# Half of a matrix's block sums move to GpSimd, and the first chunk's split, degree rows and seeds of step 0 get places of their own

## Chip, cores, metric

One core of one Trainium2 chip. The time is the device time of one execution in microseconds (us), the median of three runs. The engines are PE (TensorE), DVE (VectorE), ACT (ScalarE), POOL (GpSimd) and SP (SyncE, which here issues DMAs only).

## What is computed

A gated graph network in five steps on 2048 nodes with 256 features, with a random 0/1 adjacency matrix, then a two-layer head, a residual and a layer norm:

```python
Af = A.astype(prop_state.dtype)
AfT = Af.T
state = prop_state
for _ in range(N_STEPS):                       # 5
    s_in = state @ in_W.T + in_b
    s_out = state @ out_W.T + out_b
    a_in = Af @ s_in
    a_out = AfT @ s_out
    a = jnp.concatenate([a_in, a_out, state], axis=-1)
    r = jax.nn.sigmoid(a @ r_W.T + r_b)
    z = jax.nn.sigmoid(a @ z_W.T + z_b)
    joined = jnp.concatenate([a_in, a_out, r * state], axis=-1)
    h_hat = jnp.tanh(joined @ h_W.T + h_b)
    state = (1.0 - z) * state + z * h_hat
out = jnp.tanh(state @ o1_W.T + o1_b) @ o2_W.T + o2_b
...
x = _layernorm(x + out, axis=-1)
```

## The kernel before

The state lives in SBUF transposed (`state_t`, features on partitions, 2048 nodes in four chunks of 512). The adjacency matrix and its transpose are loaded once as int32, in 16 row blocks each (`load_rows(k)`, k from 0 to 31, on SP's queue, 1 MB each, into a ring of three stages in `tmp`), and cast by ACT to fp8 in `areg` (`cast_rows`). A load may start when the cast three rows earlier is done.

**Step 0** multiplies plainly. While the rows arrive, PE multiplies them with the state (first matrix, results "q0"; second, "p0"), with 16 matmuls to a row block, and after the last cast it finishes the p0 banks one after another. Two f16 halves are taken of each result: the upper by ACT, the lower by DVE (`lo_of_psum`). Row and column degrees come from the casts' accumulators: DVE writes them into diagonal matrices (`make_diag(d)`, 16 instructions), PE spreads them over the partitions (`spread_degrees`), and copies of that are `deg`. From `deg` ACT sets a start value in each gate bank (`seed`), and DVE adds the second matrix's part (`degree_part`). `split_hi` on ACT and `split_lo` on DVE give the halves of the state. Then `gates(0, c)` computes r, z and h for each chunk, in six tiles of 18 matmuls.

**Later steps** use Strassen's scheme on 2 x 2 blocks, which needs sums of the matrix's blocks. These don't change from step to step. They are formed once, by `matrix_sums(i)`: a job i is one pair of row blocks of one of the two matrices (0 to 7 the first, 8 to 15 the second) and takes four fp8 TENSOR_TENSORs of 128 x 1024. Its result goes to DRAM (`kept`), from where `load_group` brings each group's operands back on SP's queue. In the kernel before, DVE forms all sixteen jobs: 0 to 3 while the first matrix is loaded, 4 to 7 behind the q0 splits, 8 to 10 before `make_diag(1)`, 11 to 14 one in each chunk of `gates(0, c)`, and 15 behind them. POOL issues all the stores. Jobs 0 to 10 use three slots in `xop_words` (`ring_a`), the others two in `tmp` (`ring_b`).

Each engine runs its program in the order in which it is written, and semaphores (`wait_ge`, `then_inc`) tie them together. `s_cast` counts the casts, `s_t` the jobs.

## Time and profile before

| | |
|---|---|
| median of three runs | 1091.42 us (1090.13 to 1094.82) |
| profiled execution | 1092.24 us, its span 1090.2 us |
| PE busy | 1034.3 us of the span |
| DVE, ACT, POOL busy | 599.2, 412.0 and 37.7 us |
| granted TensorE clock, mean | 0.976 of full speed |

The span goes from the first to the last instruction. A busy share is an average over stages with different limits. The first 144 us are the loading stage, from there to about 252 us the gates of step 0 run, and the rest is four later steps and the head.

### The profile page before, as it was taken

Reading aid. Unit: us, or ns where it says so; the run is one execution under the profiler, and the core shown is the slowest. Engines: PE = TensorE matmul, PEld = TensorE weight load, DVE = VectorE, ACT = ScalarE, POOL = GpSimd, SP = SyncE. Lnnn points to the kernel's source line nnn. Section 1 sums busy time; section 2 is a strip of 40 time slices with the busy share of each in tenths; the row PEclk is TensorE's granted clock in tenths of the full one; section 3 lists DMA queues with packets and bytes.
Section 4 is the critical chain, followed back from the end, with each engine's and each line's share of the span. In section 5 each row is a group of like instructions: output and inputs, shape, how many; then the busy total and the mean of one; then the engine's idle time right before and its main releaser. Section 6 shows DMA issues by size and latency. Waiting matters only on the chain.

```text
span 1090.2 us, 11726 instructions
## 1 busy us (share of the span) xinstructions
PE 1034.3 (95%) x4776; PEld 476.2 (44%) x4776; DVE 599.2 (55%) x938; ACT 412.0 (38%) x546; POOL 37.7 (3%) x44
## 2 busy tenths in 40 slices
PE   7999979998799999999999999999999999998983
PEld 3444434443344444444444444444444444444441
DVE  5999847777244337543533664353356435355546
ACT  4655545452134116522421552242155214212431
POOL 0311000000000000000000000000000002001100
PEclk8999989999899999999999999999999999999997
DMA  9999960000630032033003301400330043000101
GB/s 344 396 368 377 385 221 20 20 20 26 283 135 1 1 145 127 1 118 152 1 1 135 136 1 69 183 20 0 135 136 1 18 184 113 1 24 15 39 1 39
DMA packets 28869, 119.63 MB, mean 110 GB/s; under 512 B 2064, under 2 KB 17040, under 8 KB 20624
## 3 DMA queue, kind: packets, MB, share of 16 engines
q1 hardware_dynamic: 26512, 110.51, 26.3%
q0 software_dynamic: 2304, 8.39, 1.9%
q8 instruction: 37, 0.61, 0.2%
q14 instruction: 16, 0.13, 0.0%
HBM read 102.11 MB, written 16.78 MB: 109 GB/s over the span
## 4 chain that ended last, share of the span: by engine, by line
PE 87%; DVE 6%; ACT 2%; DMA 2%; issue 2%; SPq 1%; DVEq 0%; ACTq 0%
PE bank L1118 41%; PE bank L1030 32%; PE bank L973 10%; PE bank L1140 1%; PE bank L1131 1%; DMA areg<-kept_operands 1%; DMA tmp<-in_adj 1%; PE bank L1159 1%; DVE areg L845 1%; DVE split L710 1%; ACT xop_words L427 0%; DVE ln_st L837 0%; DVE deg_words L699 0%; DVE tmp L634 0%; DVE tmp L631 0%
## 5 line engine op out<-in xcount | busy, mean ns | idle before, releaser
L1030 PE MATMUL bank<-areg,xop_words 128*128 128x512 fp8e4 x1792 | 393.6, 382 | 6.9 <-DMA areg<-kept_operands 5.5
L1118 PE MATMUL bank<-pq_words,w 128*128 128x512 f16 x1440 | 330.2, 382 | 0.0
L1030 PEld LDWEIGHTS bank<-areg,xop_words 128*128 128x128 f16 x1792 | 175.2, 98 | 220.5 <-DMA areg<-kept_operands 6.0
L1118 PEld LDWEIGHTS bank<-pq_words,w 128*128 128x128 f16 x1440 | 141.6, 98 | 171.2 <-issue 5.0
L435 ACT ACTIVATE tmp<-bank,bias_sb,scal 128x512 f32<-128x512 f32 x120 | 93.3, 778 | 236.6 <-PE bank L1118 228.2
L1118 PE MATMUL bank<-split,w 128*128 128x512 f16 x480 | 120.3, 388 | 15.1 <-DVE bank L735 8.2
L735 DVE SCALAR_TENSOR_TENSOR bank<-deg_words,vdeg,bank 128x512 f32<-128x512 f16 x120 | 90.0, 753 | 64.1 <-ACT bank L449 62.9
L506 ACT ACTIVATE pq_words<-pq_words 128x512 f16<-128x512 f32 x48 | 30.2, 630 | 238.3 <-DVE pq_words L886 142.0
L973 PE MATMUL bank<-areg,xop_words 128*128 128x512 fp8e4 x512 | 113.8, 386 | 3.1 <-ACT areg L375 3.1
L449 ACT ACTIVATE bank<-deg_words,vdeg 128x512 f32<-128x512 f16 x120 | 82.6, 691 | 5.4 <-DVE deg_words L699 1.7
L973 PEld LDWEIGHTS bank<-areg,xop_words 128*128 128x128 f16 x512 | 50.7, 99 | 65.6 <-issue 7.4
L1118 PEld LDWEIGHTS bank<-split,w 128*128 128x128 f16 x480 | 47.2, 99 | 70.3 <-issue 10.3
L375 ACT ACTIVATE areg<-tmp 128x2048 fp8e4<-128x2048 int32 x32 | 61.1, 1911 | 36.9 <-DMA tmp<-in_adj_t 21.5
L741 DVE TENSOR_TENSOR tmp<-tmp,state_t 128x512 f32<-128x512 f32 x40 | 27.7, 692 | 67.2 <-ACT tmp L435 67.2
L1118 PE MATMUL bank<-tmp,w 128*128 128x512 f16 x240 | 58.4, 380 | 0.0
L900 DVE SCALAR_TENSOR_TENSOR pq_words<-pq_words 128x512 f16<-128x512 f32 x48 | 33.2, 693 | 33.4 <-ACT pq_words L506 33.4
L717 DVE SCALAR_TENSOR_TENSOR xop_words<-pq_words,scal,xop_words 128x512 f16<-128x512 f32 (+1 forms) x32 | 36.8, 1151 | 25.4 <-ACT xop_words L427 25.4
L758 DVE TENSOR_TENSOR tmp<-tmp 128x512 f32<-128x512 f32 x40 | 27.6, 691 | 41.5 <-ACT tmp L435 41.5
L358 POOL TENSOR_TENSOR areg<-areg,diag_words 128x256 f32<-128x256 f32 x16 | 14.6, 942 | 735.4 <-DMA areg<-in_x 735.4
L710 DVE SCALAR_TENSOR_TENSOR split<-state_t,scal,split 128x1024 f16<-128x1024 f32 x24 | 30.7, 1283 | 12.3 <-ACT split L406 12.2
L874 DVE TENSOR_TENSOR pq_words<-bank,pq_words 128x512 f32<-128x512 f32 x16 | 11.0, 688 | 45.5 <-PE bank L1030 45.5
L1118 PEld LDWEIGHTS bank<-tmp,w 128*128 128x128 f16 x240 | 23.5, 98 | 28.3
(114 smaller groups left out, 646.6 us busy)
## 6 DMA issues: line engine op xcount, KB each, us to landing
areg<-kept_operands SPq DMA_DIRECT2D x32, 1792.0 KB, 10.7
tmp<-in_adj SPq DMA_DIRECT2D x16, 1024.0 KB, 7.3
tmp<-in_adj_t SPq DMA_DIRECT2D x16, 1024.0 KB, 8.7
kept_operands<-xop_words POOLq DMA_DIRECT2D x11, 512.0 KB, 7.9
areg<-in_x SPq DMA_DIRECT2D x8, 512.0 KB, 8.1
kept_operands<-areg SPq DMA_DIRECT2D x4, 1024.0 KB, 9.6
kept_operands<-tmp POOLq DMA_DIRECT2D x5, 512.0 KB, 3.1
pq_words<-in_gate_w SPq DMA_DIRECT2D x6, 384.0 KB, 5.8
```

What stands on the lines that cost most here:

```text
L375: nc.scalar.activation(raw8[k // JT][:, k % JT, :], stage[:, k % STG, :], ACT.Copy, accum_out=degc[:, k // JT, k % JT:k % JT + 1], saturat ...
L435: nc.scalar.activation(dst[:, gi % FT, :], gate_bank[gi % 3][:, :], ACT.Tanh if gi >= 2 * FT else ACT.Sigmoid, bias=bias_sb[:, 4 + gi:5 + ...
L449: nc.scalar.activation(gate_bank[gi % 3][:, :], deg[:, 0, cols(c)], ACT.Identity, scale=vdeg[:, 0, gi:gi + 1]).then_inc(s_c0, 1)
L506: nc.scalar.activation(dst, src, ACT.Copy, scale=PSC / XDOWN).then_inc(s_yh, 1)
L710: nc.vector.scalar_tensor_tensor(split[:, c % 2, 1, :, :], state_t[:, :, cols(c)], SIG, split[:, c % 2, 0, :, :], ALU.mult, ALU.subtract). ...
L717: nc.vector.scalar_tensor_tensor(xop[:, xs, 1, 2 * c:2 * c + 2, :], stg[:, bs, :], SIGX, xop[:, xs, 0, 2 * c:2 * c + 2, :], ALU.mult, ALU. ...
L735: nc.vector.scalar_tensor_tensor(slot, deg[:, 1, cols(c)], vdeg[:, 1, gi:gi + 1], slot, ALU.mult, ALU.add).then_inc(s_c1, 1)
L741: nc.vector.tensor_tensor(r_buf[:, f, :], r_buf[:, f, :], state_t[:, f, cols(c)], ALU.mult) \
L900: nc.vector.scalar_tensor_tensor(rows[:, 1, :], src, PSC / XDOWN, rows[:, 0, :], ALU.mult, ALU.subtract).then_inc(s_yl, 1)
L973: return nc.tensor.matmul(dst[:, :], state_n[:, j, part, feat(f)], adj8[:, j, cols(c)], start=j == 0 and part == 0, stop=j == JT - 1 and p ...
L1030: last = nc.tensor.matmul(dst[:, :], xop[:, xo, part, m, :], slot8[g % 2][:, m, mo, :], start=first and m == pairs[0] and part == 0, stop= ...
L1118: last = nc.tensor.matmul(dst[:, :], w16[:, k, wp, feat(gi)], rhs, start=False, stop=i == KT - 1 and (wp, xp) == PASSES[-1], skip_group_ch ...
```

## The change

Jobs 8 to 15 are formed by POOL (four `nc.gpsimd.tensor_tensor` each, then the store on its own queue). Jobs 8 to 12 use the second half of `state_t` as two slots (`ring_s`), so the second halves of `x_t` are loaded behind their stores, on SP's queue. Jobs 13 to 15 use `ring_b` and wait for the last cast. DVE keeps jobs 0 to 7; the stores of 4 to 7 are issued by SP, between the loads of rows 24 to 29, each behind a wait for its job. The reduction of `ow` moves ahead of the q0 splits. The split of chunk 0 moves up: on ACT behind the cast of row 26, on DVE ahead of `make_diag(1)`. ACT copies the degree rows of the first matrix and DVE those of the second; seeds wait for one bank each; and the splits of p0 for chunks 2 and 3 come behind them.

```diff
-RING_A = 11
-GATE_JOBS = len(TJOBS) - RING_A
+EARLY_JOBS = 4
+RING_S = 13
...
+        ring_s = state_t[:, :, N // 2:]
...
+        def sums_slot(i):
+            if i < PAIRS:
+                return ring_a[:, i % 3, :], s_kept_a[i], 0
+            if i < RING_S:
+                return ring_s[:, (i - PAIRS) % 2, :], s_kept_s[(i - PAIRS) % 2], (i - PAIRS) // 2
+            return ring_b[:, (i - RING_S) % 2, :], s_kept_b[(i - RING_S) % 2], (i - RING_S) // 2
+
+        def sums_parts(i):
+            d, m = TJOBS[i]
+            t = [sums_slot(i)[0].bitcast(F8).rearrange("p (h s n) -> p h s n", h=2, s=4)[:, :, s, :]
+                 for s in range(4)]
+            even, odd = [raw8[d][:, 2 * m + e, :].rearrange("p (h q n) -> p h q n", h=2, q=2) for e in range(2)]
+            return t, even, odd
+
+        def sums_home(i):
+            d, m = TJOBS[i]
+            return kept.rearrange("(h d) p m w -> d p h m w", d=2)[d][:, :, m, MT1 * CW // 4:]
...
-                if k == JT + 1:
+                if k == JT - 4:
                     sp.dma_start(ow, o_w.rearrange("(k p) m -> p k m", p=P)).then_inc(s_ow, 16)
-                if k in (11, 15, 19, 23):
-                    f, part = (k - 11) // 8, (k - 11) // 4 % 2
-                    ns = slice(part * N // 2, (part + 1) * N // 2)
-                    sp.dma_start(state_t[:, f, ns], x_t[f * P:(f + 1) * P, ns]).then_inc(s_xt[f], 16)
+                if k in (13, 15):
+                    f = (k - 13) // 2
+                    sp.dma_start(state_t[:, f, 0:N // 2], x_t[f * P:(f + 1) * P, 0:N // 2]).then_inc(s_xt[f], 16)
+                if k in (JT + 8, JT + 9, JT + 10, JT + 12):
+                    i = EARLY_JOBS + (JT + 8, JT + 9, JT + 10, JT + 12).index(k)
+                    sp.wait_ge(s_t, i + 1)
+                    sp.dma_start(sums_home(i), sums_words(i)).then_inc(sums_slot(i)[1], 16)
...
             store_raw(0)
             store_raw(1)
+            for f in range(FT):
+                for i in range(2):
+                    sp.wait_ge(s_kept_s[i], 16 * len(range(PAIRS + i, RING_S, 2)))
+                sp.dma_start(state_t[:, f, N // 2:], x_t[f * P:(f + 1) * P, N // 2:]).then_inc(s_xt[f], 16)
             sp.wait_ge(s_q0, 2 * CH)
             sp.wait_ge(s_t, PAIRS)
             sp.wait_ge(s_raw[0], 64)
+            for i in range(PAIRS):
+                sp.wait_ge(s_kept_a[i], 16)
             load_group(1, 0)
-            sp.wait_ge(s_t, 2 * PAIRS)
+            sp.wait_ge(s_tp, PAIRS)
             sp.wait_ge(s_raw[1], 64)
+                sp.wait_ge(s_kept_b[i], 16 * len(range(RING_S + i, len(TJOBS), 2)))
             load_group(1, 1)
...
-            def store_sums(i):
-                d, m = TJOBS[i]
-                to = kept.rearrange("(h d) p m w -> d p h m w", d=2)[d][:, :, m, MT1 * CW // 4:]
+            for i in range(EARLY_JOBS):
                 pool.wait_ge(s_t, i + 1)
-                if i < RING_A:
-                    nc.gpsimd.dma_start(to, ring_a[:, i % 3, :].rearrange("p (h w) -> p h w", h=2)) \
-            for i in range(PAIRS):
-                store_sums(i)
+                nc.gpsimd.dma_start(sums_home(i), sums_words(i)).then_inc(sums_slot(i)[1], 16)
             pool.wait_ge(s_mx, 3)
             nc.gpsimd.partition_all_reduce(mall[:, 3:5], mx[:, 3:5], P, RMAX).then_inc(s_mall, 1)
+
+
             for i in range(PAIRS, len(TJOBS)):
-                store_sums(i)
+                (t1, t2, t3, t4), even, odd = sums_parts(i)
+                slot, kept_sem, uses = sums_slot(i)
+                n = i - PAIRS
+                pool.wait_ge(s_cast, JT + 2 * n + 2)
+                if i == RING_S:
+                    pool.wait_ge(s_cast, 2 * JT)
+                if uses > 0:
+                    pool.wait_ge(kept_sem, 16 * uses)
+                nc.gpsimd.tensor_tensor(t1, even[:, :, 1, :], even[:, :, 0, :], ALU.subtract, saturate=False) \
+                    .then_inc(s_tcp, 1)
+                nc.gpsimd.tensor_tensor(t3, odd[:, :, 1, :], even[:, :, 1, :], ALU.subtract, saturate=False)
+                pool.wait_ge(s_tcp, 2 * n + 1)
+                nc.gpsimd.tensor_tensor(t2, odd[:, :, 1, :], t1, ALU.subtract, saturate=False).then_inc(s_tcp, 1)
+                pool.wait_ge(s_tcp, 2 * n + 2)
+                nc.gpsimd.tensor_tensor(t4, odd[:, :, 0, :], t2, ALU.subtract, saturate=False).then_inc(s_tp, 1)
+                pool.wait_ge(s_tp, n + 1)
+                nc.gpsimd.dma_start(sums_home(i), sums_words(i)).then_inc(kept_sem, 16)
...
-            for k in range(JT + 1, 2 * JT):
-                cast_rows(k)
-            for c in range(CH):
-                for f in range(FT):
-                    act.wait_ge(s_p0, 2 * c + f + 1)
-                    nc.scalar.activation(pq[:, c, f, 0, :], bank[p0_bank(c, f)][:, :], ACT.Copy, scale=PSC) \
-                        .then_inc(s_p0h, 1)
-
 
             def split_hi(c, at, new):
+                if at == 0:
+                    for f in range(FT):
+                        act.wait_ge(s_xt[f], 16)
+                if at == 2:
+                    for f in range(FT):
+                        act.wait_ge(s_xt[f], 32)
...
+            for k in range(JT + 1, 2 * JT):
+                cast_rows(k)
+                if k == JT + 10:
+                    split_hi(0, 0, 0)
             act.wait_ge(s_bias, 16)
-            act.wait_ge(s_deg, 2 * CH)
+            for c in range(CH // 2):
+                for f in range(FT):
+                    p0_hi(c, f)
+            for c in range(CH):
+                act.wait_ge(s_dg, c + 1)
+                nc.scalar.copy(deg[:, 0, cols(c)], bank[4 + c][:, :]).then_inc(s_deg_in, 1)
+            act.wait_ge(s_deg_in, CH)
             for gi in range(3):
+                act.wait_ge(s_deg_out, gi + 1)
                 seed(0, 0, gi)
-            for f in range(FT):
-                act.wait_ge(s_xt[f], 32)
-            split_hi(0, 0, 0)
+            for c in range(CH // 2, CH):
+                for f in range(FT):
+                    p0_hi(c, f)
...
             def matrix_sums(i):
-                d, m = TJOBS[i]
-                words = ring_a[:, i % 3, :] if i < RING_A else ring_b[:, (i - RING_A) % 2, :]
-                dve.wait_ge(s_cast, JT * d + 2 * m + 2)
-                if 3 <= i < RING_A:
-                    dve.wait_ge(s_kept_a[i % 3], 16 * (i // 3))
-                if i >= RING_A + 2:
-                    dve.wait_ge(s_kept_b[(i - RING_A) % 2], 16 * ((i - RING_A) // 2))
-                nc.vector.tensor_tensor(t1, even[:, :, 1, :], even[:, :, 0, :], ALU.subtract, saturate=False).then_inc(s_tc, 1)
+                (t1, t2, t3, t4), even, odd = sums_parts(i)
+                dve.wait_ge(s_cast, 2 * i + 2)
+                if i >= 3:
+                    dve.wait_ge(s_kept_a[i - 3], 16)
+                nc.vector.tensor_tensor(t1, even[:, :, 1, :], even[:, :, 0, :], ALU.subtract, saturate=False) \
+                    .then_inc(s_tc, 1)
...
-            for c in range(CH):
-                for f in range(FT):
-                    dve.wait_ge(s_q0h, 2 * c + f + 1)
-                    lo_of_psum(c, FT + f, bank[2 * c + f], s_q0l)
-            for i in range(4, PAIRS):
-                matrix_sums(i)
-            make_diag(0)
-
             dve.wait_ge(s_ow, 16)
             nc.vector.tensor_reduce(mx[:, 3:4], ow[:, :, 0:D], mybir.AxisListType.XY, ALU.max,
                                     apply_absolute_value=True)
             nc.vector.tensor_reduce(mx[:, 4:5], ow[:, :, D:2 * D], mybir.AxisListType.XY, ALU.max,
                                     apply_absolute_value=True).then_inc(s_mx, 1)
+
+            for c in range(CH):
+                for f in range(FT):
+                    dve.wait_ge(s_q0h, 2 * c + f + 1)
+                    lo_of_psum(c, FT + f, bank[2 * c + f], s_q0l)
+            for i in range(EARLY_JOBS, PAIRS):
+                matrix_sums(i)
+            make_diag(0)
+
...
-            for i in range(PAIRS, RING_A):
-                matrix_sums(i)
-            make_diag(1)
-
-            def p0_lo(c, f):
-                dve.wait_ge(s_p0h, 2 * c + f + 1)
-                lo_of_psum(c, f, bank[p0_bank(c, f)], s_p0l)
-
-            def deg_out(d):
-                for c in range(CH):
-                    dve.wait_ge(s_dg, CH * d + c + 1)
-                    nc.vector.tensor_copy(deg[:, d, cols(c)], bank[4 + c][:, :]).then_inc(s_deg, 1)
-
-            for c in range(CH):
-                p0_lo(c, 0)
-                if c >= CH - 2:
-                    deg_out(c - (CH - 2))
-                p0_lo(c, 1)
-            dve.wait_ge(s_deg, 2 * CH)
-
             def split_lo(c, at):
                 dve.wait_ge(s_sph, at + 1)
                 nc.vector.scalar_tensor_tensor(split[:, c % 2, 1, :, :], state_t[:, :, cols(c)], SIG,
                                                split[:, c % 2, 0, :, :], ALU.mult, ALU.subtract).then_inc(s_spl, 1)
+
+            split_lo(0, 0)
+            make_diag(1)
+
+            def p0_lo(c, f):
+                dve.wait_ge(s_p0h, 2 * c + f + 1)
+                lo_of_psum(c, f, bank[p0_bank(c, f)], s_p0l)
+
+            for c in range(CH // 2):
+                for f in range(FT):
+                    p0_lo(c, f)
+            for c in range(CH):
+                dve.wait_ge(s_dg, CH + c + 1)
+                nc.vector.tensor_copy(deg[:, 1, cols(c)], bank[4 + c][:, :]).then_inc(s_deg_out, 1)
+            dve.wait_ge(s_deg_out, CH)
...
                 keep_part(n, c, 1)
-                if t == 0:
-                    for i in range(RING_A + c, RING_A + c + 1):
-                        matrix_sums(i)
...
-            split_lo(0, 0)
+            for c in range(CH // 2, CH):
+                for f in range(FT):
+                    p0_lo(c, f)
             for c in range(CH):
                 gates(0, c)
-                if c == CH - 1:
-                    for i in range(RING_A + CH, len(TJOBS)):
-                        matrix_sums(i)
...
                     else:
-                        pe.wait_ge(s_deg, c + 1)
+                        pe.wait_ge(s_deg_in, c + 1)
                     nc.tensor.matmul(bank[4 + c][:, :], ones[:, :], diag[d][:, c * JC:(c + 1) * JC, :],
                                      start=True, stop=True).then_inc(s_dg, 1)
```

On SP, between the loads of the second matrix, before (the rows of `in_adj_t` are rows 16 to 31; `x_t` goes to `state_t`):

```order
L250 DMA tmp<-in_adj_t 128x2048 [waits s_cast] x2
L264 DMA state_t<-in_x_t 128x1024
L250 DMA tmp<-in_adj_t 128x2048 [waits s_cast] x4
L264 DMA state_t<-in_x_t 128x1024
L250 DMA tmp<-in_adj_t 128x2048 [waits s_cast] x8
L274 DMA kept_operands<-areg 1024x1x128 [waits s_cast]
```

and after, with the four stores of DVE's jobs (`kept_operands<-xop_words`) among the loads:

```order
L274 DMA tmp<-in_adj_t 128x2048 [waits s_cast] x9
L291 DMA kept_operands<-xop_words 128x2x512 [waits s_t]
L274 DMA tmp<-in_adj_t 128x2048 [waits s_cast]
L291 DMA kept_operands<-xop_words 128x2x512 [waits s_t]
L274 DMA tmp<-in_adj_t 128x2048 [waits s_cast]
L291 DMA kept_operands<-xop_words 128x2x512 [waits s_t]
L274 DMA tmp<-in_adj_t 128x2048 [waits s_cast] x2
L291 DMA kept_operands<-xop_words 128x2x512 [waits s_t]
L274 DMA tmp<-in_adj_t 128x2048 [waits s_cast] x3
L301 DMA kept_operands<-areg 1024x1x128 [waits s_cast]
```

The two late loads of `state_t` are gone from here. Four waits for `s_t` stand ahead of the last seven loads.

On DVE, from the last sums or the splits of the output weights (`o`) to the first gate seeds, before:

```order
L634 TENSOR_TENSOR xop_words<-areg,xop_words 128x2x512 [waits s_tc]
L636 TENSOR_TENSOR xop_words<-areg,xop_words 128x2x512 [waits s_tc]
L645 TENSOR_SCALAR tmp<-ident,degc 128x128 [waits s_cast]
L645 TENSOR_SCALAR tmp<-ident,degc 128x128 x15
L639 SCALAR_TENSOR_TENSOR pq_words<-bank,pq_words 128x512 [waits s_p0h] x5
L699 CAST deg_words<-bank 128x512 [waits s_dg] x4
L639 SCALAR_TENSOR_TENSOR pq_words<-bank,pq_words 128x512 [waits s_p0h] x2
L699 CAST deg_words<-bank 128x512 [waits s_dg] x4
L639 SCALAR_TENSOR_TENSOR pq_words<-bank,pq_words 128x512 [waits s_p0h]
L735 SCALAR_TENSOR_TENSOR bank<-deg_words,vdeg,bank 128x512 [waits s_c0,s_deg]
L735 SCALAR_TENSOR_TENSOR bank<-deg_words,vdeg,bank 128x512 [waits s_c0] x2
L710 SCALAR_TENSOR_TENSOR split<-state_t,scal,split 128x1024 [waits s_sph]
```

and after:

```order
L664 SCALAR_TENSOR_TENSOR o<-deg_words,scal,o 128x2x256 [waits s_wh]
L736 SCALAR_TENSOR_TENSOR split<-state_t,scal,split 128x1024 [waits s_sph]
L690 TENSOR_SCALAR tmp<-ident,degc 128x128 [waits s_cast]
L690 TENSOR_SCALAR tmp<-ident,degc 128x128 x15
L684 SCALAR_TENSOR_TENSOR pq_words<-bank,pq_words 128x512 [waits s_p0h] x4
L751 CAST deg_words<-bank 128x512 [waits s_dg] x4
L776 SCALAR_TENSOR_TENSOR bank<-deg_words,vdeg,bank 128x512 [waits s_c0,s_deg_out]
L776 SCALAR_TENSOR_TENSOR bank<-deg_words,vdeg,bank 128x512 [waits s_c0] x2
L684 SCALAR_TENSOR_TENSOR pq_words<-bank,pq_words 128x512 [waits s_p0h] x4
```

The split of chunk 0 (`split<-state_t`) went from behind the seeds to ahead of the diagonal matrix (`tmp<-ident,degc`). One of two sets of degree copies (CAST) stays, the sums (`xop_words<-areg,xop_words`) are gone, and half of the p0 splits follow the seeds.

On POOL, behind the first four stores, before (the all-reduce is the ISA row):

```order
L335 ISA areg<-areg 128x1536 [waits s_vpart]
L342 DMA kept_operands<-xop_words 128x2x512 [waits s_t] x8
L351 ISA mall<-mx 128x2 [waits s_mx]
L342 DMA kept_operands<-xop_words 128x2x512 [waits s_t] x3
L345 DMA kept_operands<-tmp 128x2x512 [waits s_t] x5
```

and after, the first of eight jobs:

```order
L367 DMA kept_operands<-xop_words 128x2x512 [waits s_t] x4
L369 ISA mall<-mx 128x2 [waits s_mx]
L381 ISA
L381 TENSOR_TENSOR state_t<-areg 128x2x512 [waits s_cast]
L383 TENSOR_TENSOR state_t<-areg 128x2x512
L385 TENSOR_TENSOR state_t<-areg,state_t 128x2x512 [waits s_tcp]
L387 TENSOR_TENSOR state_t<-areg,state_t 128x2x512 [waits s_tcp]
L389 DMA kept_operands<-state_t 128x2x512 [waits s_tp]
```

Stores that only waited for DVE have become POOL's own sums, each with its store behind it.

## Rows read from the trace of the kernel before

**Rows 1.** The page: each engine's busy time and share of the span.

```profile
PE 1034.3 (95%) x4776; PEld 476.2 (44%) x4776; DVE 599.2 (55%) x938; ACT 412.0 (38%) x546; POOL 37.7 (3%) x44
```

**Rows 2.** Stretch: us, busy PE, PEld, DVE, ACT, POOL; clock, DMA share, GB/s.

```profile
100.00:110.00 10.00, 10.00 (x48) 4.50 (x47) 9.01 (x35) 4.56 (x5) 1.09 (x2) 1.00 1.02 427
```

**Rows 3.** Timeline of ACT (start, us, what): two casts.

```profile
79.59 1.90 ACT L375 ACTIVATE areg<-tmp 128x2048 fp8e4<-128x2048 int32 x1
...
125.03 1.91 ACT L375 ACTIVATE areg<-tmp 128x2048 fp8e4<-128x2048 int32 x1 [2.65 <-DMA tmp<-in_adj_t]
```

**Rows 4.** The chain of waits, 120 to 150 us (start, us, what).

```profile
131.76 0.60 ACT pq_words L397
...
142.18 1.29 DVE split L710
```

**Rows 5.** Timeline of PE, with idle time before and what ended it.

```profile
143.60 2.72 PE L1118 MATMUL bank<-split,w 128*128 128x512 f16 x6 [6.82 <-DVE split L710]
...
150.37 1.46 PE L1118 MATMUL bank<-split,w 128*128 128x512 f16 x6
...
200.33 2.45 PE L1118 MATMUL bank<-split,w 128*128 128x512 f16 x6 [2.31 <-DVE bank L735]
...
252.44 1.12 PE L1131 MATMUL bank<-ident,state_t 128*128 128x128 f32 x4 [3.29 <-DVE state_t L761]
...
285.37 14.89 PE L1030 MATMUL bank<-areg,xop_words 128*128 128x512 fp8e4 x59 [5.47 <-DMA areg<-kept_operands]
```

**Rows 6.** Timelines of SP's queue and of POOL: issues of DMAs.

```profile
116.44 0.33 SPq L250 DMA_DIRECT2D tmp<-in_adj_t  x1
...
274.19 6.54 SPq L283 DMA_DIRECT2D areg<-kept_operands  x4
...
270.91 0.72 POOL L345 DMA_DIRECT2D kept_operands<-tmp  x1 [18.82 <-DVE tmp L636]
```

**Rows 7.** Timeline of DVE in the loading stage.

```profile
76.76 4.88 DVE L639 SCALAR_TENSOR_TENSOR pq_words<-bank,pq_words 128x512 f16<-128x512 f32 x8
81.55 1.22 DVE L631 TENSOR_TENSOR xop_words<-areg 128x1024 fp8e4<-128x1024 fp8e4 x1
82.68 1.23 DVE L632 TENSOR_TENSOR xop_words<-areg 128x1024 fp8e4<-128x1024 fp8e4 x1
...
101.02 2.69 DVE L645 TENSOR_SCALAR diag_words<-ident,degc 128x128 f16<-128x128 f16 x16
...
110.11 1.22 DVE L631 TENSOR_TENSOR xop_words<-areg 128x1024 fp8e4<-128x1024 fp8e4 x1
```

**Rows 8.** Timelines of POOL and of DVE around 914 us.

```profile
0.24 0.10 POOL L1217 MEMSET const-float32-0.0<- 128x1 f32 x1 [0.24 <-issue]
...
913.41 0.72 POOL L358 TENSOR_TENSOR areg<-areg,diag_words 128x256 f32<-128x256 f32 x1
914.09 1.18 POOL L358 TENSOR_TENSOR areg<-areg,diag_words 128x256 f32<-128x256 f32 x1
915.23 1.17 POOL L358 TENSOR_TENSOR areg<-areg,diag_words 128x256 f32<-128x256 f32 x1
...
914.71 1.10 DVE L761 TENSOR_TENSOR state_t<-tmp 128x512 f32<-128x512 f32 x1
...
918.53 0.69 DVE L761 TENSOR_TENSOR state_t<-tmp 128x512 f32<-128x512 f32 x1
```

**Rows 9.** DVE beside POOL, by timeline, and the page's line of L735.

```profile
910.76 0.76 DVE L735 SCALAR_TENSOR_TENSOR bank<-deg_words,vdeg,bank 128x512 f32<-128x512 f16 x1 [0.40 <-ACT bank L449]
...
983.62 0.43 DVE L823 TENSOR_SCALAR pq_words<-pq_words 128x512 f16<-128x512 f32 x1 [4.00 <-ACT pq_words L482]
...
984.70 0.95 DVE L823 TENSOR_SCALAR pq_words<-pq_words 128x512 f16<-128x512 f32 x1
...
37.46 6.59 DVE L604 TENSOR_TENSOR scal<-scal,mall 128x1 f32<-128x1 f32 x1
...
L735 DVE SCALAR_TENSOR_TENSOR bank<-deg_words,vdeg,bank 128x512 f32<-128x512 f16 x120 | 90.0, 753 | 64.1 <-ACT bank L449 62.9
```

More of the change, by code:

```diff
@@ L160, in gnn_program @@
         s_p0, s_p0h, s_p0l = sem("s_p0"), sem("s_p0h"), sem("s_p0l")
-        s_diag, s_dg, s_deg = sem("s_diag"), sem("s_dg"), sem("s_deg")
-        s_tc, s_t = sem("s_tc"), sem("s_t")
-        s_kept_a = [sem(f"s_kept_a{i}") for i in range(3)]
+        s_diag, s_dg, s_deg_in, s_deg_out = sem("s_diag"), sem("s_dg"), sem("s_deg_in"), sem("s_deg_out")
+        s_tc, s_t, s_tcp, s_tp = sem("s_tc"), sem("s_t"), sem("s_tcp"), sem("s_tp")
+        s_kept_a = [sem(f"s_kept_a{i}") for i in range(PAIRS)]
         s_kept_b = [sem(f"s_kept_b{i}") for i in range(2)]
+        s_kept_s = [sem(f"s_kept_s{i}") for i in range(2)]
         s_raw = [sem("s_raw0"), sem("s_raw1")]
@@ L421, in rows_hi @@
                     if n == 0:
-                        for i in range(3):
-                            act.wait_ge(s_kept_a[i], 16 * len(range(i, RING_A, 3)))
+                        for i in range(PAIRS):
+                            act.wait_ge(s_kept_a[i], 16)
                 else:
@@ L646, in make_diag @@
                 last.then_inc(s_diag, 1)
-            for i in range(4):
+            for i in range(EARLY_JOBS):
                 matrix_sums(i)
@@ L686, in _, with split_lo @@
                 split_raw(3 + i, [o16[:, :, h, ms] for h in range(2)], ow[:, :, ms], om)
-            for i in range(PAIRS, RING_A):
-                matrix_sums(i)
+            def split_lo(c, at):
+                dve.wait_ge(s_sph, at + 1)
+                nc.vector.scalar_tensor_tensor(split[:, c % 2, 1, :, :], state_t[:, :, cols(c)], SIG,
+                                               split[:, c % 2, 0, :, :], ALU.mult, ALU.subtract).then_inc(s_spl, 1)
+            split_lo(0, 0)
             make_diag(1)
@@ L1126, in transposes @@
                 if n == 0 and f == 0:
-                    pe.wait_ge(s_deg, 2 * CH)
+                    pe.wait_ge(s_deg_out, CH)
                     pe.wait_ge(s_id32, 1)
```

23 lines of the change are left out of this document (6 added, 17 removed).

## The prediction

> **What bounds the kernel now.** I read the engines' busy time first. TensorE (PE) is busy 95% of the span [rows 1], so only what makes PE wait, or a gap that closes, can move the time. The change touches the first 300 us, so I read that part by stretches. From 100 to 110 us, as in the stretches around it, PE is busy throughout, DVE nine tenths, and the DMA engines are saturated (share 1.02 at 427 GB/s) [rows 2]: adjacency rows arrive, ACT casts them, PE multiplies them. The three run neck and neck. The last cast starts at 125.03 and ends at 126.9 [rows 3], and PE's last block of the stage can only start then.
>
> Then I read the chain of waits from 130 to 144 us and PE's idle time. Behind the last block stand degree copies, seeds and the split of chunk 0, one after another on DVE and ACT [rows 4], and PE idles 6.8 us before its first gate matmul at 143.60 [rows 5]. It then runs at its lower clock: six matmuls take 2.72 us where six take 1.46 later [rows 5], which is about 3 us over the first tile. Inside step 0 PE waits 2.3 us (once more like it, at 228.68) and 3.3 us for what DVE does behind `matrix_sums` [rows 5]. At 285.37 it waits 5.5 us for the load of group 1 [rows 5], which SP issued at 274.19, after the last job had been stored at 270.91 [rows 6]. So about 17 us of idle time plus some 5 us of slow clock lie open: 22 us at most.
>
> **What the change moves, without any interference.** The eight jobs of the second matrix leave DVE. A job there is four TENSOR_TENSORs at 1.13 us from start to start [rows 7], 4.6 us. Three of them stood before the end of the stage, where DVE had slack anyhow, and four stood in step 0. The split of chunk 0, the seeds and half of the degree copies leave the gap: the chain after the last block shrinks from 11.9 us to about 7, of which PE's last block covers most. I put the gates at 139.8 instead of 143.6 (the moved reduction of `ow`, 1.3 us for two of them, sits before the eight q0 splits, which hold PE's next pass, and costs 0.9 us). Step 0 loses another 6 us of waits, and the wait at 285 goes with its slow clock after it (59 matmuls in 14.89 us, where 48 took 10.00 [rows 2] and 59 would take 12.5): 7.5 us. The sum is -3.8 - 6 - 7.5, about -17 us.
>
> **What POOL costs.** No row shows POOL on fp8. The nearest are its 256-element additions: 0.72 us alone at 913.41, the next starting 0.68 us later [rows 8]. Four times that gives 2.7 us for a 1024-element instruction. Less if a part is fixed: a one-element MEMSET takes 0.10 [rows 8], so (0.68 - 0.1) x 4 + 0.1 = 2.4. A job on POOL is then 4 x 2.3 plus 0.72 for its DMA issue, 10 us, against 4.6 on DVE. From the cast that job 8 needs (the one from 79.59 to 81.5 [rows 3]) five jobs end near 131, three more near 161. `load_group(1, 1)` and the second halves of `state_t` (needed some 40 us into the gates) are in time. By itself the slower engine is hidden.
>
> **What is not hidden: the two engines block each other.** The same POOL additions took 1.18 and 1.17 us when DVE worked on SBUF beside them, and the DVE instruction between them 1.10 instead of 0.69 [rows 8]. They follow one another strictly: POOL's starts are 914.09 and 915.23, 1.14 apart instead of 0.68. The DVE instruction holds about half of the 1.13 that one of twice the elements takes [rows 7], which leaves 0.57 to POOL. Instructions with one operand in PSUM are free of it (L735 took 0.76 while POOL worked, its mean over all 120 is 753 ns) [rows 9]. A TENSOR_SCALAR from SBUF to SBUF is not: 0.95 against 0.43 [rows 9]. Even a one-element TENSOR_TENSOR waited 6.59 us beside the all-reduce [rows 9]. And `make_diag`'s sixteen, 2.69 us together [rows 7], are of the TENSOR_SCALAR kind.
>
> The Trainium skill ("SBUF — State Buffer", section "Who interferes with whom") has this as a rule: a DVE instruction with two SBUF inputs, or one in a two-port mode, excludes a GpSimd instruction that reads SBUF, and whichever comes second is blocked until the first ends. By this rule, the trace agrees, the change's two streams of block sums run in turn and not side by side; without the blocking the sum would be the -17 us above, with it the +17 below. The skill's "GPSIMD Engine Reference" (section 3) gives 4497 ns for a 2048-element addition there; an estimate from it is 2.3 us for 1024, which would leave the sum as it is.
>
> For 1024 elements POOL's hold is 0.57 x 4 = 2.3 us, or 0.1 + 0.47 x 4 = 2.0 with a fixed part; I take 2.1. DVE holds 1.1. One turn of both is 3.2 us.
>
> Now the chain. (1) DVE comes to job 4 at 82.9 (81.6 and the 1.3 of the moved reduction), POOL to job 8 at 81.5. Each of DVE's sixteen instructions of jobs 4 to 7 waits for one of POOL's: the jobs end at 94.5, 107, 120 and 133. Before, the last of the four ended where `make_diag(0)` starts, at 101.0 [rows 7]. (2) SP now waits for just these jobs between adjacency loads. Load 26 now stands behind job 5 (107), 27 and 28 behind job 6 (120), 29 to 31 behind job 7 (133). Before, the last was issued at 116.44 and had 8.6 us to its cast [rows 3, 6]; three loads and two stores, 4 MB, take 10 us at 427 GB/s and 2 to land: the last cast ends at 147, 20 us late. (3) DVE goes on from 133 with the sixteen of `make_diag(0)`, and POOL's job 12 puts four turns between them: 133 + 2.6 + 8.4 = 144 less what has run already, 143. Scales and `o16` splits (what lies between the end of `make_diag(0)` and 110.11 [rows 7], less the moved reduction: 5.1 us) bring it to 148, the split of chunk 0 to 151. (4) At the last cast, 147, POOL starts jobs 13 to 15, just as DVE comes to `make_diag(1)`. Of POOL's twelve instructions about seven fall between DVE's twenty-one short ones: 148 + 1.2 + 2.6 + 7 x 2.1 = 166. (5) PE waits there for the second degree rows. Behind it on DVE come four splits (2.4), four degree copies (2.4), a seed on ACT (0.7) and its other half (0.8), with 1.5 for semaphores and matmuls: the gates start at 174, 30 us later than at 143.6. (6) Then -6 us in step 0 and -7.5 at the wait for group 1: 30 - 13.5 = 16.5 us.
>
> PE loses its clock in the long waits, but what it then does slowly lies under DVE's chain, and the first gate tile was slow before as well, so I add nothing. The profiled execution has a span of 1090.2 and a time of 1092.24, 0.8 over the median of 1091.42. **1092.2 + 16.5 is 1109 us.** The sum is steep: 16 + 4 + 7 = 27 POOL instructions lie on the path, so a hold of 2.0 gives 1105, of 2.3 gives 1121, and at 1.5 the change breaks even.
>
> **Rivals.** *No blocking* (fp8 work or its modes don't meet): all is hidden and the sum is -17, 1075 us. For it: what met in the trace was f32 and f16, not fp8. Against it: [rows 8, 9]. Chance 0.20. *POOL's fp8 instructions are short*, 1.0 to 1.4 us, since four elements share a word: same turns, jobs 4 to 7 end by 116 to 121, last cast 131 to 137, and the sum is -10 to -3: 1082 to 1089. No row speaks for it. 0.08. *Only long instructions block*, and the short ones of `make_diag` slip through between POOL's: steps 1 and 2 stand, 3 and 4 shrink to 151 for the second diagonal, the gates start at 159: +15 - 13.5, 1088 to 1099. For it: instructions of 0.16 us beside POOL's pause between two. 0.14. *POOL needs 3 us or more* for fp8 conversions: over 1126, with state halves that then arrive late too. 0.04. My forecast, 1100 to 1126, has 0.54.
>
> The bound for a real difference is 0.5% (1086 and 1097). Faster: the first rival and some of the second, 0.25. Same: the rest of it and half of the third, 0.12. Slower: 0.63. With cases of both signs the range reaches from 1077 to 1125, which leaves out half of the first rival, the last one, and the edge of my own.
>
> **What would show it.** In the changed profile: POOL's TENSOR_TENSORs, alone 2.2 to 2.7 us, beside DVE 3.2 apart; DVE's sums 3.2 us from start to start at 84 to 133 (step 1); SP's loads of `in_adj_t` with idle time behind DVE's sums, last cast near 147 (2); `make_diag` stretched from 2.7 to 10 us or more (3, 4); the first gate matmul near 174 (5); no wait for `kept_operands` in group 1, and step 0 without the 2 us waits (6). If DVE's sums stay 1.13 apart I am wrong from step 1 on; if SP's loads are on time, in step 2.

## Result and the profile after

The changed kernel takes 1111.74 us (median of four runs, 1111.67 to 1112.68) against 1093.05 for the kernel before on the same chip (1090.13 to 1094.82). The ratio is 1.0176 with a 95% interval of [1.0148, 1.0203]: slower by 1.8%, 18.7 us. The profiled execution took 1111.69 us with a span of 1109.9.

The page answers to [rows 1]: TensorE's share of the span falls from 95% to 93%, since its own work is the same and the span longer; POOL's busy time grows by 66.5 us.

```profile
PE 1030.0 (93%) x4776; PEld 474.2 (43%) x4776; DVE 618.0 (56%) x902; ACT 413.5 (37%) x550; POOL 104.2 (9%) x72
```

The next table is that of the stretches (us, busy time of PE, PEld, DVE, ACT and POOL; PE clock, DMA share, GB/s) of the changed kernel, cut at the end of the q0 splits, the last casts, the first gate matmul and the end of step 0.

```profile
78.00:127.00 49.00, 38.93 (x176) 16.56 (x174) 48.90 (x21) 19.61 (x21) 40.85 (x21) 0.95 0.61 219
127.00:153.00 26.00, 14.77 (x49) 5.72 (x50) 19.60 (x38) 10.01 (x10) 9.80 (x6) 0.71 0.87 309
153.00:187.00 34.00, 12.14 (x42) 4.31 (x41) 29.53 (x25) 7.50 (x13) 25.48 (x15) 0.70 0.96 337
187.00:283.00 96.00, 96.00 (x460) 45.34 (x458) 60.56 (x88) 54.20 (x74) 0.00 (x0) 1.00 0.09 37
283.00:316.00 33.00, 32.71 (x155) 14.87 (x154) 14.22 (x21) 9.11 (x13) 0.00 (x0) 1.00 0.20 78
```

Of the 109 us from 78 to 187 PE works 66, and DVE is recorded as busy for 98, in the first stretch with 21 instructions in 49 us; time in which an instruction stands and waits for the other engine counts as busy here. The DMA share, 1.02 from 100 to 110 us before [rows 2], is 0.61 over the first stretch: it is no longer the loads that are short of bandwidth. From 187 on PE has no gap at all. The same view of the kernel before, for step 0 and what follows:

```profile
144.00:252.00 108.00, 100.54 (x456) 45.79 (x454) 73.92 (x97) 53.14 (x71) 2.82 (x4) 0.96 0.12 48
252.00:286.00 34.00, 27.54 (x122) 12.55 (x123) 19.20 (x26) 7.25 (x10) 0.81 (x2) 0.90 0.41 160
```

DVE's timeline in the changed kernel (start, us, what; in brackets idle time before and what ended it) shows the sums that [rows 7] has at 1.22 us each:

```profile
83.88 1.21 DVE L679 TENSOR_TENSOR xop_words<-areg,xop_words 128x1024 fp8e4<-128x1024 fp8e4 x1
85.13 2.91 DVE L681 TENSOR_TENSOR xop_words<-areg,xop_words 128x1024 fp8e4<-128x1024 fp8e4 x1
87.97 3.02 DVE L675 TENSOR_TENSOR xop_words<-areg 128x1024 fp8e4<-128x1024 fp8e4 x1
...
96.91 7.14 DVE L681 TENSOR_TENSOR xop_words<-areg,xop_words 128x1024 fp8e4<-128x1024 fp8e4 x1
103.98 3.02 DVE L675 TENSOR_TENSOR xop_words<-areg 128x1024 fp8e4<-128x1024 fp8e4 x1
106.93 7.06 DVE L677 TENSOR_TENSOR xop_words<-areg 128x1024 fp8e4<-128x1024 fp8e4 x1
...
137.95 2.68 DVE L690 TENSOR_SCALAR diag_words<-ident,degc 128x128 f16<-128x128 f16 x16
```

POOL's timeline in the same kernel:

```profile
84.55 2.41 POOL L381 TENSOR_TENSOR state_t<-areg 128x1024 fp8e4<-128x1024 fp8e4 x1 [7.17 <-issue]
...
97.03 2.02 POOL L381 TENSOR_TENSOR state_t<-areg 128x1024 fp8e4<-128x1024 fp8e4 x1
99.00 2.01 POOL L383 TENSOR_TENSOR state_t<-areg 128x1024 fp8e4<-128x1024 fp8e4 x1
100.96 2.00 POOL L385 TENSOR_TENSOR state_t<-areg,state_t 128x1024 fp8e4<-128x1024 fp8e4 x1
103.04 2.88 POOL L387 TENSOR_TENSOR state_t<-areg,state_t 128x1024 fp8e4<-128x1024 fp8e4 x1
106.22 0.73 POOL L389 DMA_DIRECT2D kept_operands<-state_t  x1 [0.30 <-POOL state_t L387]
```

Read the two side by side. DVE's instruction of 96.91 "takes" 7.14 us: it stands there while POOL's of 97.03, 99.00 and 100.96 run, and gets its 1.13 us in ahead of the one of 103.04, which stands itself for that time (2.88 us instead of 2.01). The next one comes in behind that one, at POOL's store. So DVE gets two instructions into each of POOL's jobs of 9.93 us, at the two places where POOL itself waits for something (ahead of its fourth instruction, and for its store), and none between POOL's first three. Between 85 and 96 us it was different: there POOL's instructions took 2.9 to 3.0 us as well and the two engines alternated. The traces of this kernel and of the experiments below that leave POOL's order as it is (x1, x2, y2, y3, z2) sort the two patterns, with one exception: in a job that POOL begins straight behind its store, 0.02 or 0.03 us later, DVE's waiting instruction is passed over, and in a job that POOL begins after a pause of 1 us or more (job 8, later job 13, in x1 job 15) it is let in after one. The exception is y3's job at 171.95. Why it is so, the traces don't show.

The chain of waits, up to the first gate matmul (start, us, what; "issue" is time in which the trace shows no reason to wait):

```profile
136.81 1.24 DVE xop_words L681
...
138.06 0.38 SPq L291
...
139.85 10.51 DMA tmp<-in_adj_t
...
150.38 2.01 ACT areg L411 x2
...
152.41 24.20 DVE tmp L690 x16
...
184.91 1.90 issue
186.81 31.24 PE bank L1155 x144
```

These seven lines hold the delay of the first gate matmul: the last job of DVE ends at 138, SP stores it and issues the last three loads, which before had gone out by 116.44 [rows 6]; they come in, the last cast ends at 152.3 (126.9 before), and `make_diag(1)` takes 24.20 us where sixteen such instructions took 2.69 [rows 7]. The view of its line gives the shortest, median and longest of the sixteen in ns:

```profile
L690 DVE TENSOR_SCALAR tmp<-ident,degc x16: 241/248/6569, 152.4 to 170.0; 128x128 f16<-128x128 f16 x16
```

So most of them pay nothing. One by one, nine took 0.24 or 0.25 us, five 1.99 to 2.04 (one POOL instruction) and two 6.57 (three POOL instructions in a row). PE's timeline, which answers to [rows 5]:

```profile
132.40 8.50 PE L1010 MATMUL bank<-areg,xop_words 128*128 128x512 fp8e4 x32 [15.44 <-ACT areg L411]
...
177.36 2.38 PE L1050 MATMUL bank<-diag_words,ones 128*128 128x512 f16 x4 [19.91 <-DVE pq_words L684]
179.53 3.62 PE L1010 MATMUL bank<-areg,xop_words 128*128 128x512 fp8e4 x8
...
186.81 1.46 PE L1155 MATMUL bank<-split,w 128*128 128x512 f16 x6 [1.90 <-issue]
...
282.67 0.60 PE L1168 MATMUL bank<-ident,state_t 128*128 128x128 f32 x4
```

The gates start 43.2 us late (186.81 against 143.60). Step 0, up to the first transpose behind its gates, takes 95.9 us against 108.8: 13.0 back. The rest of the span takes 827.2 against 837.8: 10.6 back. 43.2 - 13.0 - 10.6 is 19.6 us; the spans differ by 19.7.

### The profile page after: what moved, and what is told of

Same layout as the page of the kernel before. It is cut to its first block, busy times and chain, and to the rows that moved or that the text cites. A ratio compares the mean times of both kernels' runs of the same rounds, so it can differ in the third digit from the quotient of the medians.

```text
span 1109.9 us, 11731 instructions
## 1 busy us (share of the span) xinstructions
PE 1030.0 (93%) x4776; PEld 474.2 (43%) x4776; DVE 618.0 (56%) x902; ACT 413.5 (37%) x550; POOL 104.2 (9%) x72
## 4 chain that ended last, share of the span: by engine, by line
PE 79%; DVE 14%; issue 3%; DMA 2%; ACT 1%; SPq 1%; POOL 0%; DVEq 0%
PE bank L1155 42%; PE bank L1067 33%; DVE tmp L690 2%; DVE xop_words L677 2%; DVE xop_words L675 1%; DVE xop_words L679 1%; PE bank L1168 1%; PE bank L1177 1%; DMA tmp<-in_adj_t 1%; PE bank L1196 1%; DMA areg<-in_x 1%; DVE scal L654 1%; DVE areg L883 1%; DVE xop_words L631 1%; DVE w L664 0%
## 5 line engine op out<-in xcount | busy, mean ns | idle before, releaser
L1155 PE MATMUL bank<-split,w 128*128 128x512 f16 x480 | 118.0, 382 | 5.5 <-DVE bank L776 3.6
L799 DVE TENSOR_TENSOR tmp<-tmp 128x512 f32<-128x512 f32 x40 | 27.8, 695 | 43.2 <-ACT tmp L469 43.2
L461 ACT ACTIVATE xop_words<-pq_words,scal 128x512 f16<-128x512 f32 (+1 forms) x32 | 33.1, 1036 | 7.0 <-DVE pq_words L771 6.5
## 6 DMA issues: line engine op xcount, KB each, us to landing
areg<-kept_operands SPq DMA_DIRECT2D x32, 1792.0 KB, 10.6
```

Of the source, the lines that this page charges most:

```text
L461: nc.scalar.activation(xop[:, xs, 0, 2 * c:2 * c + 2, :], stg[:, bs, :], ACT.Identity, scale=SIGX) \
L1155: last = nc.tensor.matmul(dst[:, :], w16[:, k, wp, feat(gi)], rhs, start=False, stop=i == KT - 1 and (wp, xp) == PASSES[-1], skip_group_ch ...
```

## Experiments

| kernel | us | ratio to before, same chip | gates start |
|---|---|---|---|
| after | 1111.74 | 1.0176 [1.0148, 1.0203] | 186.8 |
| x1_late13 | 1090.25 | 0.9974 [0.9959, 0.9989] | 163.8 |
| x2_stores_behind | 1108.81 | one run | 184.3 |
| x3_pool_writes | 1076.32 | one run | 151.8 |
| x4_pool_chained | 1103.03 | one run | 178.5 |
| y1_chain_only | 1084.50 | 0.9932 [0.9909, 0.9955] | 138.2 |
| y2_pool_five_late | 1075.20 | 0.9848 [0.9822, 0.9874] | 140.1 |
| y3_pool_after_dve | 1088.77 | 0.9970 [0.9953, 0.9987] | 162.4 |
| z1_five_late_chained | 1074.42 | 0.9833 [0.9808, 0.9858] | 138.1 |
| z2_five_late_again | 1077.21 | 0.9866 [0.9842, 0.9890] | 138.0 |

x2, x3 and x4 have one run each, so what is read from them rests on their traces and not on a few us of their times.

My theory, A: DVE's and POOL's instructions exclude each other on SBUF, and both the late loads and the 24 us of `make_diag(1)` come from it. Rivals: the loss is SP's new waits by themselves; or POOL's traffic slows DVE whatever POOL does; or POOL passes DVE over only because its instructions stand back to back (C).

**x1: jobs 13 to 15 wait for `make_diag(1)`.**

```diff
                 if i == RING_S:
                     pool.wait_ge(s_cast, 2 * JT)
+                    pool.wait_ge(s_diag, 2)
```

> One wait added to the changed kernel: POOL starts job 13 only when the second diagonal matrix is done. Theory A (POOL's instructions on SBUF shut out DVE's two-input and two-port ones): the sixteen diagonal writes take 2.7 us again instead of 24.2, the first gate matmul comes at 165 to 169 instead of 186.8, and jobs 13 to 15 then stretch DVE's work in step 0 by 2 to 6 us: 1093 to 1099 us. Theory B (POOL is merely slow, and DVE's instructions are long for another reason, such as the DMA traffic of that stretch, which stays): the diagonal writes stay near 24 us and the time near 1111.

DVE's timeline:

```profile
152.15 2.69 DVE L691 TENSOR_SCALAR tmp<-ident,degc 128x128 f16<-128x128 f16 x16 [5.26 <-ACT areg L412]
```

One wait, on an engine whose results nobody needs yet, gives back 21.5 us: `make_diag(1)` is at its old 2.69, the gates start at 163.8, and the kernel is 0.3% faster than the one before, some 3 us better than I had expected. The last cast ends at 152.0, as late as in the changed kernel. The three jobs now run beside the first chunk of step 0, where the longest DVE instruction they stretched took 2.36 us. So the cost of `make_diag(1)` is that of POOL's jobs beside it.

**x2: SP stores jobs 4 to 7 behind the last load**, so no load waits for a job.

```diff
-                if k in (JT + 8, JT + 9, JT + 10, JT + 12):
-                    i = EARLY_JOBS + (JT + 8, JT + 9, JT + 10, JT + 12).index(k)
+                if k == 2 * JT - 1:
+                  for i in range(EARLY_JOBS, PAIRS):
```

> The changed kernel with the four stores of jobs 4 to 7 issued by SP behind the last load, so that no load waits for a job. Theory A: the last cast ends at 127 to 130 instead of 152, but DVE's jobs still end near 138 and POOL's jobs 13 to 15 now fall on both diagonal matrices and the splits, so the first gate matmul stays within 180 to 192 and the time within 1104 to 1118. Theory B2 (SP's waits are the whole loss): gates from 160 on, 1085 to 1092.

```profile
139.05 26.36 DVE L690 TENSOR_SCALAR diag_words<-ident,degc 128x128 f16<-128x128 f16 x16
...
171.23 2.68 DVE L690 TENSOR_SCALAR tmp<-ident,degc 128x128 f16<-128x128 f16 x16
```

The last cast ends at 122.9, 29 us earlier, and the gates start only 2.5 us earlier. POOL's jobs 13 to 15 now begin as soon as job 12 is stored, at 139, and meet the first `make_diag` instead of the second. Without SP's waits the loads are in time, but this takes away one of two delays of the same origin, and the other one stands. The rival "SP's waits by themselves" falls. The edit has a price of its own: job 7 waits 5.96 us, at 122.29, for the late store of the slot that it writes to, and the 2.5 us hold this too.

**x3: POOL only writes.** Its four subtractions become four MEMSETs into the same places (the sums of the second matrix are left out and zeros stored; the rest is as in the changed kernel).

```diff
-                nc.gpsimd.tensor_tensor(t1, even[:, :, 1, :], even[:, :, 0, :], ALU.subtract, saturate=False) \
-                    .then_inc(s_tcp, 1)
+                nc.gpsimd.memset(first, 0.0).then_inc(s_tcp, 1)
...
```

> POOL's 32 subtractions are replaced by 32 MEMSETs of 2048 fp8 elements each (the sums of the second matrix are left out, zeros are stored). Theory A with the rule that only reads of POOL meet DVE's second input: DVE's sums of jobs 4 to 7 take 1.14 us each again and end near 101 to 105, the loads are in time, while the second diagonal (a two-port kind) is still stretched if POOL's MEMSETs are about 2 us long: 1075 to 1095. Theory A2 (any POOL instruction on SBUF shuts out any of these on DVE): sums of 3 to 7 us as in the changed kernel and 1105 to 1112. Theory B (traffic, not the engines): no change in DVE's durations, 1105 to 1112.

DVE's timeline, then POOL's:

```profile
90.24 1.22 DVE L683 TENSOR_TENSOR xop_words<-areg,xop_words 128x1024 fp8e4<-128x1024 fp8e4 x1
91.38 1.22 DVE L677 TENSOR_TENSOR xop_words<-areg 128x1024 fp8e4<-128x1024 fp8e4 x1
...
105.17 17.18 DVE L692 TENSOR_SCALAR diag_words<-ident,degc 128x128 f16<-128x128 f16 x16
...
128.17 15.08 DVE L692 TENSOR_SCALAR tmp<-ident,degc 128x128 f16<-128x128 f16 x16
```

```profile
90.91 1.82 POOL L384 MEMSET state_t<- 128x2048 fp8e4 x1
92.65 1.82 POOL L386 MEMSET state_t<- 128x2048 fp8e4 x1
```

POOL's four instructions of a job stand back to back, and DVE's subtractions keep their 1.22 us and 1.14 from start to start. The TENSOR_SCALARs do not: 17 and 15 us. So it is not the DMA traffic, which is heavier here (a share of 0.99 from 78 to 127 us) than in the changed kernel (0.61). Two kinds of DVE instruction meet POOL: one with two SBUF inputs meets POOL's subtractions but not its MEMSETs, which read nothing, and the TENSOR_SCALAR meets both. The time of 1076 is no forecast, since the kernel leaves out the sums, but the gates still start 8 us later than in the kernel before, with the last cast on time (127.3) and only `make_diag` stretched.

The Trainium skill ("SBUF — State Buffer", section "Who interferes with whom") states both halves: two SBUF inputs contend with a GpSimd instruction that reads, "not with one that only writes it", and TENSOR_SCALAR can enter the two-port modes, which contend with either. By this rule, the trace agrees: 1.22 us against 3.02, and 17 us against 2.69.

**x4: each POOL subtraction waits for the one before**, so that none stands back to back.

```diff
+                pool.wait_ge(s_tcp, 3 * n + 1)
                 nc.gpsimd.tensor_tensor(t3, odd[:, :, 1, :], even[:, :, 1, :], ALU.subtract, saturate=False)
...
```

> The changed kernel, but each of POOL's four subtractions waits for the one before it. In the changed kernel DVE gets in only where POOL has a wait of its own (before the fourth instruction and at the store), three POOL instructions late otherwise. Theory C (POOL holds on from one instruction to the next when nothing holds it back): DVE gets in behind every instruction, turns of 3.1 us, jobs 4 to 7 end near 134 instead of 138 with no instruction of 7 us, the second diagonal takes 15 to 26 us, 1104 to 1112. Theory D (who comes next has nothing to do with POOL's waits): instructions of 7 us stay.

```profile
109.18 3.04 DVE L683 TENSOR_TENSOR xop_words<-areg,xop_words 128x1024 fp8e4<-128x1024 fp8e4 x1
112.15 3.02 DVE L677 TENSOR_TENSOR xop_words<-areg 128x1024 fp8e4<-128x1024 fp8e4 x1
115.09 3.02 DVE L679 TENSOR_TENSOR xop_words<-areg 128x1024 fp8e4<-128x1024 fp8e4 x1
...
153.31 15.62 DVE L692 TENSOR_SCALAR tmp<-ident,degc 128x128 f16<-128x128 f16 x16
```

The 7 us instructions are gone. DVE and POOL take strict turns of 2.95 us, and the four jobs end at 124 instead of 138, ten us before my forecast for this run. This is the turn-taking that the prediction assumed, and waits between POOL's instructions make it last. C holds so far: with the waits DVE is never passed over. Without them it isn't always, so standing back to back is not the whole condition. `make_diag(1)` shrinks to 15.6 (again seven of the sixteen wait, but each for one POOL instruction), but `make_diag(0)` now meets POOL as well (15.6 us), and so do the splits between the two. In all 8.7 us come back, a little more than I had expected.

**y1: the chain part of the change alone**, put into the kernel before: split, degree rows, seeds and p0 splits in their new places, all jobs on DVE, loads and stores as they were.

```diff
+                if k == JT + 10:
+                    for f in range(FT):
+                        act.wait_ge(s_xt[f], 32)
+                    split_hi(0, 0, 0)
...
+            split_lo(0, 0)
             make_diag(1)
```

> The kernel before with the chain part of the change alone: the split of chunk 0, the degree rows (one matrix on ACT, one on DVE), the seeds' waits and the late half of the p0 splits have their new places; all sixteen jobs stay on DVE where they were, POOL computes nothing, loads and stores are as before. Theory A (all the loss comes from POOL beside DVE, the chain part is sound): first gate matmul near 140 instead of 143.6 and at the full clock, step 0 and the wait for group 1 as before: 1083 to 1088 us. Rival (the chain part loses too, or hides nothing): 1091 or more.

PE's timeline:

```profile
138.24 1.46 PE L1128 MATMUL bank<-split,w 128*128 128x512 f16 x6 [1.91 <-issue]
...
192.09 1.47 PE L1128 MATMUL bank<-split,w 128*128 128x512 f16 x6 [2.31 <-DVE bank L743]
...
276.70 27.27 PE L1040 MATMUL bank<-areg,xop_words 128*128 128x512 fp8e4 x112 [5.16 <-DMA areg<-kept_operands]
```

This part is a gain: 6.8 us, gates 5.4 us earlier and at full clock (six matmuls in 1.46 us; 2.72 before [rows 5]). The waits of step 0 (2.31, 2.31 and 3.29 us) are those of [rows 5] and the one for group 1 is 5.16 us (5.47 there), so they belong to the jobs.

**y3: POOL starts job 8 only when DVE's job 7 is done**, and job 13 after `make_diag(1)`; otherwise the changed kernel.

```diff
+            pool.wait_ge(s_t, PAIRS)
             for i in range(PAIRS, len(TJOBS)):
...
                     pool.wait_ge(s_cast, 2 * JT)
+                    pool.wait_ge(s_diag, 2)
```

> The changed kernel, but POOL starts job 8 only when DVE has done job 7, and job 13 when the second diagonal is done. Theory A: DVE's sums take 1.14 us each and end near 105, SP's loads are in time, last cast 126 to 130; POOL's jobs 8 to 12 (105 to 155) now stretch both diagonals, the second by 15 to 25 us, so that the first gate matmul comes at 155 to 168: 1080 to 1091. If instead the sums or loads are still late, the blocking of DVE's sums was not what held SP's loads: 1090 or more.

```profile
105.01 24.49 DVE L692 TENSOR_SCALAR diag_words<-ident,degc 128x128 f16<-128x128 f16 x16
...
132.28 6.77 DVE L666 SCALAR_TENSOR_TENSOR o<-deg_words,scal,o 128x512 f16<-128x512 f32 x1
...
141.90 7.07 DVE L738 SCALAR_TENSOR_TENSOR split<-state_t,scal,split 128x1024 f16<-128x1024 f32 x1
```

The loads are on time again (last cast 126.0), the jobs too (105), and yet the gates start at 162.4: now `make_diag(0)`, a split of `o` and the split of chunk 0 pay. So five POOL jobs between 105 and 150 cost time as well: much of what DVE does there is of the kind that meets POOL.

**y2: y1 and POOL forms jobs 11 to 15 behind `make_diag(1)`.** These are the five jobs that stood in step 0 on DVE.

```diff
-                if t == 0:
-                    for i in range(RING_A + c, RING_A + c + 1):
-                        matrix_sums(i)
...
+            pool.wait_ge(s_cast, 2 * JT)
+            pool.wait_ge(s_diag, 2)
+            for i in range(RING_A, len(TJOBS)):
...
```

> The run y1 with jobs 11 to 15, which stand in step 0 on DVE's path, moved to POOL, which starts them when the second diagonal matrix is done (near 130). They end near 180. Theory A: DVE's two-input instructions of step 0 are stretched by up to 6 us where they meet POOL, but PE has slack there; the waits of 2.3 us in step 0 and that of 5.5 us for group 1 go: 1068 to 1076. Rival: the blocking in step 0 falls on PE's path (r, z and the state's update) and eats the gain: 1080 to 1092.

1075.20 us, 1.5% faster than before. PE has no wait for group 1 any more, and two waits are left in step 0, of 5.67 and 2.92 us, each behind a DVE instruction that three of POOL's passed over. That left one thing to try.

**z1: y2, and each POOL subtraction waits for the one before** (the edit of x4). **z2** is y2 once more, on the same chip.

> The kernel with the chain part and five late POOL jobs, but each POOL subtraction now waits for the one before it. If POOL lets DVE in only where it really waits itself, DVE's SBUF subtractions in step 0 that took 7.06 and 6.40 us (three POOL instructions) take at most 3.0 each, TensorE's waits of 5.67 and 2.92 us at 173 and 182 shrink to 1 or 2 us, and the time falls by 3 to 8 us against the same kernel without these waits, to 1067 to 1073 us. POOL's own pace may slow, from 9.4 to 11 or 12 us a job, still long before its results are needed. Rival: DVE is passed over for another reason, say because two POOL reads queue ahead whatever they wait for. Then the 7 us instructions stay and the time is 1075 within 0.3%.

> The kernel with the chain part and five late POOL jobs once more, unchanged, on the same chip as the one with the added waits, so that the two ratios can be compared. 1075 us, ratio 0.985 within 0.002.

DVE's timeline in z2, PE's in z2, then both in z1:

```profile
164.33 6.94 DVE L791 TENSOR_TENSOR state_t<-tmp 128x512 f32<-128x512 f32 x1
```

```profile
171.99 2.74 PE L1144 MATMUL bank<-split,w 128*128 128x512 f16 x6 [6.64 <-DVE bank L765]
...
181.38 1.47 PE L1144 MATMUL bank<-split,w 128*128 128x512 f16 x6 [2.61 <-DVE bank L765]
```

```profile
163.29 3.04 DVE L793 TENSOR_TENSOR state_t<-tmp 128x512 f32<-128x512 f32 x1
```

```profile
167.05 1.47 PE L1146 MATMUL bank<-split,w 128*128 128x512 f16 x6 [1.61 <-DVE bank L767]
...
180.42 1.09 PE L1159 MATMUL bank<-ident,state_t 128*128 128x128 f32 x4 [4.48 <-ACT pq_words L429]
```

No DVE instruction of this stretch is above 3.04 us any more, and PE's waits of 6.64 and 2.61 become 1.61 and 0.33, but one of 4.48 appears at 180: DVE is now slowed a little at more places. The medians differ by 2.8 us (1074.42 and 1077.21), less than the 3 to 8 that I had expected, z1 is above the 1067 to 1073 of my forecast, and the intervals of the ratios overlap. The mechanism is seen in the trace; that it gains time rests on those two medians. With 1.7% it is the fastest kernel of this study.

## Where the prediction was right and where wrong

Direction and size were right, 1109 us against 1111.7 and +16.5 against +18.7. Several steps were off, in both directions:

| step | predicted | measured |
|---|---|---|
| 1. jobs 4 to 7 end | 94.5, 107, 120, 133 | 88.0, 104.0, 123.9, 138.0 |
| 2. last cast ends | 147 | 152.3 |
| 3. `make_diag(0)` | stretched to 143 | 2.68 us, ends 140.6 |
| split of chunk 0 ends | 151 | 146.5 |
| 4. `make_diag(1)` ends | 166 | 176.6 |
| 5. gates start | 174 (+30) | 186.8 (+43.2) |
| 6. step 0 | -6 | -13.0 |
| rest | -7.5 | -10.6 |

**Step 1** had the right cause and nearly the right end, by a form that was wrong. I let the engines take turns, 3.2 us for each. In fact POOL's instruction is shorter (2.01 us alone, 1.96 from start to start; I took a hold of 2.1), and a turn is 2.95. But from 96.9 on POOL's first three instructions of a job give no turn: two DVE instructions in 9.93 us make 5.0 for each. POOL also started its first job at 84.55 and not at 81.5, which let DVE's first three instructions through at full speed. x4, where turns are strict, measured what step 1 describes, with 124 for its end. A slip stands in the slope as well: with 27 POOL instructions on the path a hold of 2.3 us gives 1114, not 1121.

**Step 2** followed from step 1: 5 us later there, 5 us later here. x2 shows that, with the rest in place, it was worth little (2.5 us, and a new wait beside it).

**Step 3** did not happen. By the time of `make_diag(0)` POOL had finished job 12 (its store is issued at 135.99) and was waiting for the last cast.

**Step 4** is the mis-sized term: I counted seven POOL instructions between DVE's, eleven of the twelve ran before `make_diag(1)` was done (24.2 us instead of about 17). Seven of DVE's sixteen did wait, but two of them for three POOL instructions each, which makes 5 + 6 = 11. In x4, where each wait was for one, the sixteen took 15.6 us. I had shared POOL's turns among twenty-one instructions from 148 on; the five before `make_diag(1)` had run by 146.5, and its sixteen started with POOL's twelve, at 152.4 and 152.5. x1 takes this one term away and gave back 21.5 us.

**Step 5**: from the end of `make_diag(1)` to the gates it took 10.2 us where I had 7.8. I added nothing for PE's clock, and this was wrong: behind the wait of 19.9 us PE's four spreads took 2.38 us and eight last matmuls 3.62, where x1, whose last wait there was 4.1 us, took 1.18 and 1.89. This is 2.9 us on the chain.

**Step 6** was too small. The waits of 2.31, again 2.3 and 3.29 us go, 7.9 us; I had 6. And the clock in step 0, which I had left out, rose from 0.96 to 1.00 of its full 2.4 GHz (the stretches above), an estimated 4 us of 108. For the rest, 6.5 us of idle time in 252 to 286 and a clock of 0.90 there (an estimated 3.4 us) make 9.9 of the 10.6. So the later steps gave back 10 us more than I thought, the chain had cost 13 more, and the sum stayed close: part of the agreement is luck.

No run has the changed kernel without interference, so the term of -17 us was not measured itself. What comes nearest are y2 and z1, other kernels, which keep POOL off the chain up to the gates and measure -16.1 and -17.6 against the kernel before. Of the rivals, "no blocking" is refuted by x1, x3 and x4. "Only long instructions block" was half right and fails by the other half: nine of the sixteen short ones slipped through, as it said, and the seven others cost 21.5 us. "Short fp8 instructions" and "3 us or more" fall by 2.01 us.

## What to carry to other kernels

Before moving element-wise work from DVE to POOL, list what DVE runs beside it by its operands: two inputs in SBUF, or SBUF-to-SBUF TENSOR_SCALARs, waited here for whole POOL instructions, one or three at a time. A row of short ones doesn't pay once for each (nine of sixteen paid nothing), but it moves on only as fast as POOL's work does: 2.69 us became 24. Put the POOL work where nothing on DVE's chain is due, with a wait for the DVE step that must not be touched; here that one wait was worth 21 us, and choosing the jobs of step 0 instead of those of the loading stage made a loss of 18.7 us a gain of 16. Where they must meet, a semaphore wait between POOL's instructions is worth trying, since in x4 and z1 it handed DVE its turn.
